# Taking an eighth of the edges' source rows from SBUF columns in every pair, and GpSimd's wait one gather later

## What is computed

```python
msg_in = concatenate([nodes[src], nodes[dst], edge_features], axis=-1)
messages = relu(msg_in @ mW1 + mb1) @ mW2 + mb2
aggregated = segment_sum(messages, dst)
upd_in = concatenate([nodes, aggregated], axis=-1)
out = layernorm(nodes + relu(upd_in @ uW1 + ub1) @ uW2 + ub2)
```

## Time and profile before

| | |
|---|---|
| median of three runs | 2489.68 us (2489.13 to 2490.9) |
| the profiled execution | 2490.1 us |
| its span in the profile | 2488.3 us |
| PE / PEld busy | 62% / 57% |
| POOL busy | 59% |
| DVE busy | 45% |
| ACT busy | 39% |
| granted TensorE clock, mean | 0.72 |

### The profile page before, as it was taken

How to read it: one execution, slowest core, us unless ns; L and a number is a source line. 1 busy time by engine, 2 the same in 40 slices (tenths; PEclk the granted TensorE clock), 3 DMA queues, 4 the chain that set the end, 5 groups by cost and what they waited for, 6 DMA issues and landing times. The chain is left out here.

```text
span 2488.3 us, 35326 instructions
## 1 busy us (share of the span) xinstructions
PE 1553.6 (62%) x8744; PEld 1428.1 (57%) x8744; DVE 1114.3 (45%) x4860; ACT 972.5 (39%) x6697; POOL 1475.7 (59%) x1576
## 2 busy tenths in 40 slices
PE   2676666665666666576666666567566566557657
PEld 2566655555565565565565565556566555556555
DVE  3435445444444444444444444444444444444443
ACT  1215334334334434443433433443433444443342
POOL 7155566666656666566666565665656666666653
PEclk6787776776766866766767777776766777676776
DMA  4634434333334333333333343343333343333331
GB/s 109 179 91 108 98 81 99 97 85 92 98 80 98 97 90 90 96 96 83 97 94 85 95 99 83 95 99 80 97 96 85 93 99 94 84 98 93 86 91 33
DMA packets 102736, 232.74 MB, mean 94 GB/s; under 512 B 47018, under 2 KB 63223, under 8 KB 89917
## 3 DMA queue, kind: packets, MB, share of 16 engines
q1 hardware_dynamic: 42532, 124.03, 19.9%
q0 software_dynamic: 49952, 100.83, 16.4%
q10 hardware_dynamic: 10046, 5.59, 0.9%
HBM read 220.66 MB, written 9.60 MB: 93 GB/s over the span
## 5 line engine op out<-in xcount | busy, mean ns | idle before, releaser
L797 POOL DMA_INDIRECT gath<-table_src,idx_all x1513 | 1427.6, 944 | 970.9 <-issue 873.0
L932 PE MATMUL ps_sum<-onehot,hid 128*128 128x96 f32 x3322 | 598.4, 353 | 628.0 <-ACT rhs L1065 535.8
L932 PEld LDWEIGHTS ps_sum<-onehot,hid 128*128 128x128 f32 x3322 | 563.4, 263 | 664.2 <-issue 659.8
L516 ACT COPY col_x<-xz 64x1 f32 x5960 | 634.9, 187 | 409.5 <-issue 403.9
L912 PE MATMUL ps_pre<-rhs,lhs 128*128 128x128 f32 x3226 | 593.7, 360 | 222.6 <-issue 164.3
L1298 DVE TENSOR_TENSOR hid<-ps_pre,gath 128x1024 f32<-128x1024 f32 x202 | 246.7, 1221 | 1067.3 <-DMA gath<-table_src,idx_all 925.6
L912 PEld LDWEIGHTS ps_pre<-rhs,lhs 128*128 128x128 f32 x3226 | 560.6, 270 | 244.1 <-issue 179.4
L1103 ACT ACTIVATE hid<-hid 128x1024 f32<-128x1024 f32 x202 | 212.7, 1053 | 358.9 <-DVE hid L1298 356.1
L539 DVE TENSOR_TENSOR col_x<-xz 64x2 int32 x3366 | 265.2, 148 | 81.5 <-issue 78.6
L1269 DVE TENSOR_SCALAR_CACHE_REDUCE lhs<-lhs,place 96x1024 f32<-96x1024 int32 x208 | 262.6, 1263 | 62.9 <-PE ps_sum L845 32.5
L1261 DVE TENSOR_TENSOR onehot<-ps_iota,dst_rel 128x768 f32<-128x768 f32 (+1 forms) x209 | 196.8, 942 | 0.1
(11 more groups left out here) (136 smaller groups left out, 672.6 us busy)
## 6 DMA issues: line engine op xcount, KB each, us to landing
lhs<-in_dst_dram SPq DMA_DIRECT2D x99, 768.0 KB
lhs<-in_edgeT_dram SPq DMA_DIRECT2D x98, 256.0 KB
gath<-table_src,idx_all POOLq DMA_INDIRECT x1513
table_src<-gath SPq DMA_DIRECT2D x12, 512.0 KB, 5.3
xwin<-in_xT_dram SPq DMA_DIRECT2D x208, 24.0 KB
lhs<-in_dst_dram SPq DMA_DIRECT2D x10, 384.0 KB
out_dram<-late_b ACTq DMA_DIRECT2D x48, 64.0 KB, 2.7
xz<-in_xT_dram ACTq DMA_DIRECT2D x4, 512.0 KB, 5.1
```

The costliest lines, as they stand in the source:

```text
L516: ins = copy(col_x[:, k, start + n + j:start + n + j + 1], col)
L797: pool.indirect_dma_start(gath[0:m, k, j * H:(j + 1) * H], None, table_src, src_by_tile(p, j, m)).then_inc(gathered[k], 16)
L932: nc.tensor.matmul(bank[:, 0:WIN], hid[0:m, k, j * H:(j + 1) * H], hot(k, j, m), start=(j == 0), stop=(m == TAIL or j == PT - 1))
```

## The change

Two edits. `COL_EVERY` becomes 1, so that each of the 197 pairs from 11 to 207 has one tile by columns and gathers only seven (the last pair three). All that depends on `has_cols(p)` follows from it: ACT copies 60 columns and DVE makes 34 joins in each step, the first 12 registers of the next pair are loaded by ACT behind the columns of the same step and ahead of `copy_window`, and the counts that semaphores are waited for go with them. And POOL now issues the first gather of a pair as soon as the slot is free; its wait for the gathers of the pair ahead stands between the first and the second gather.

```diff
-COL_EVERY = 2
+COL_EVERY = 1
...
-                if p > RAW:
-                    pool.wait_ge(gathered[(k - 1) % SLOTS], got(p - 1))
                 let(pool)
-                for j, m in tiles_of(p)[0:gathers_of(p)]:
+                for n, (j, m) in enumerate(tiles_of(p)[0:gathers_of(p)]):
+                    if n == 1 and p > RAW:
+                        pool.wait_ge(gathered[(k - 1) % SLOTS], got(p - 1))
+                        let(pool)
                     pool.indirect_dma_start(gath[0:m, k, j * H:(j + 1) * H], None, table_src, src_by_tile(p, j, m)).then_inc(gathered[k], 16)
```

## The result

The changed kernel took **2762.4 us** (2759.3 to 2777.6, four runs), the kernel before in the same comparison 2490.3 (2489.1 to 2495.5). The ratio is **1.109, interval 1.103 to 1.114**: slower by 272 us. The forecast was 2629.

A forecast was written before the change was run, and what follows sets the result against it. POOL was taken to set the pace now, ACT nearly as late; after the change ACT's step of 12.2 us replaces 11.49 over 196 steps, adding 139 us to 2490.1 for 2629 us. Range 2340 to 2780.

The forecast's parts named there:

- ACT sets the pace, slower than before: The forecast case: ACT's step of 12.2 us is longer than POOL's 9.5, DVE's and PE's; chance 0.59.
- the crawl: In ACT's batch, the slow supply of small instructions while gathers are in flight; 4.2 us of each batch.
- The marks named in advance: Signs in the profile after: slot releases POOL's first gather, relu hardly idle, 11,840 copies, batch near 10.6 us, relus 12.2 apart.
- the 10.6 forecast: ACT's batch of 60 column copies, busy and idle time together, taken from the profile before at 10.6 us.
- ACT's step: ACT's work per pair: batch 10.6, relu 1.06, `rhs` copy 0.16, node update 0.4; sum 12.2 us.
- the quarter of a node update: Term of ACT's step: L1152 at 0.47 and squares about 1.0, a quarter of them a pair, 0.4 us.
- a register load priced at 0.74 us: Upper cost of ACT's moved load of the next pair's first 12 registers; step 12.95 us, time 2776.
- The register load taken at 0: ACT's load of the next pair's first 12 registers, behind queued copies ahead of the `rhs` copy, costs 0.
- The wait edit "is worth nothing" if ACT sets the pace: With ACT setting the pace, POOL waits for the slot, not the landing, so moving its wait gains nothing.
- Register-addressed columns whose registers are not loaded yet come slowly: Inference for ACT's batch while gathers are in flight: nine columns took 0.6 us each, the others about 0.1.
- the rival given 0.09, POOL keeps the pace: If the crawl nearly vanishes, ACT's step is 9.6 us, POOL's 9.5, and time 2118 us; chance 0.09.
- the 0.78 worked out: What stays of POOL's 2.03 us wait once the first gather (1.25 us) runs inside it: 0.78 us.

The follow-up runs named there:

- Fixed columns: The changed kernel, but ACT copies its 60 columns from fixed places of xz and loads no registers for them; 2070.3 us without the crawl, 2751.2 with it.
- every other pair, no wait: The kernel before without POOL's wait for the landings of the preceding pair's gathers, columns still in every other pair; 2906.5 us, ratio 1.171, with the crawl.
- wait only: The changed kernel with columns in every other pair, so that only POOL's wait is moved; 2207.5 us, ratio 0.883, without the crawl.
- cols only: The kernel before with columns in every pair, POOL's wait left ahead of a pair's first gather; 2331.6 us, ratio 0.930, without the crawl.
- no wait: The changed kernel without POOL's wait for the gathers of the pair ahead, only the free slot gating; 1859.4 us, ratio 0.744, without the crawl.

## Why the prediction was right, and by what it was right

**ACT sets the pace, slower than before: right, and with luck,** in both comparisons with the crawl (ratios 1.109 and 1.120). The marks named in advance are there: the slot as releaser of POOL's first gather, a relu without idle time ahead, 11,840 copies, a batch of 10.98 us against the 10.6 forecast. The luck is that the comparison had the crawl, like the profile that the forecast was made from; in the two later ones without it in which it ran, the changed kernel was faster than the kernel before by 17 to 18%.

**The size was short by 133 us**, against the profiled 2777.6 by 149. The step of the sum that was mis-sized is ACT's step, 12.97 us for 12.2, and 196 x 0.77 = 151. Half is the batch: + 0.38. The other half is the quarter of a node update, forecast at 0.4: ahead of L1153 and L1161, ACT is idle for 23.9 + 29.5 us, 0.35 us a pair, mostly with a releaser that the profile can't name. The upper end of the range, 2780, held the time by 18 us, and it stood for another cause: a register load priced at 0.74 us, which the runs don't show.

**The register load taken at 0: right.** Without the crawl a batch with five loads and 60 registers takes 5.66 us with no idle time that can be seen in it, and kernels whose ACT loads none in the loop cost the same (2070 and 2078 beside 2065). The trace also records the loads themselves, which the views leave out: the five of a batch take 3.99 us together, 66 ns a register, with the crawl as without it, and run beside the copies. The Trainium skill ("Runtime: NRT & Kernel Launch", section "Instruction fetch mechanics") gives some 200 ns a register, in a remark on the loads that the runtime adds. The prediction carried it over to these loads from a table in SBUF, where 60 would take 12 us; the 3.99 us show that it does not hold for them.

**The wait edit "is worth nothing" if ACT sets the pace: not shown, and perhaps too kind.** The moved wait was not run alone with the crawl. But the whole wait taken away from the kernel before cost 428 us there: the pause at each landing was worth more to the other engines than it cost POOL, and no term of the sum held that.

**What failed is a premise:** that the crawl in the one profile of before belongs to the kernel. "Register-addressed columns whose registers are not loaded yet come slowly" was inferred from coinciding times. `Fixed columns` with the crawl shows that it is neither ACT's register loads nor its addressing, and PE in `every other pair, no wait` that it isn't ACT alone. And three of the five later comparisons had no crawl. There the rival given 0.09, POOL keeps the pace at 2118 us, is what happened, at 2061 to 2065, and its sums hold: `wait only` was to save 1.25 us a pair, 245 us, and saved 291; `cols only` was to come to 10.77 us a pair and came to 11.1 (1006 gathers in 1600 us are 143.7 pairs). The rest of the wait is 1.05 to 1.25 us idle, 0.30 of it the usual gap, so 0.75 to 0.95 for the 0.78 worked out.

**Why before's time hid it.** With the crawl the kernel before took 2478 and 2490 us, without it 2498 to 2503. POOL's chain of gathers and landings was its bound either way, and ACT's 10.6 us batch fitted beside it in two steps. But the near-equal times are two differences that cancel. With the crawl the start is slower: the first relu with columns comes at 184.95 us, without it at 116.88, 68 us sooner. And the steady stretch is quicker: 172 relus in 2000 us, 11.63 us a pair, for 167 and 11.98. The gathers cost POOL 7.5 x 1.248 = 9.36 us of either, so a landing was waited for some 0.3 us longer without the crawl; why, no run shows. The change takes POOL's wait and ACT's empty step together, so that the time becomes that of ACT: 12.97 us a pair where a batch crawls, 9.75 (POOL again) where it takes 5.66.

**What stays open** is how the crawl works and what makes it come and go; nothing in the programs provoked it. One candidate is the supply of instructions. They come by DMA: the two instruction queues moved 1.73 + 1.26 = 2.99 MB for 46,113 instructions, 65 bytes each. The Trainium skill (the same page and section) says that each sequencer fetches its next block through a DMA queue of its own while it executes the current one. One might argue from it that gathers crowd out these fetches, so that an engine slows once its block is used up. For that speaks that the crawl begins late: in the earlier trace rows 4.6 us after a burst starts (gathers from 1508.72, the first gap ahead of 1513.79), and ACT, after 15.84 us of rest, still makes 18 copies at full speed 20.6 us into the burst of `every other pair, no wait`.

The trace of the result speaks against it. From 1508.9 ACT's copies come in bunches of one to four, and then it makes 49 at full speed. Here are these 49, and all that DMA did from 1508.6 to 1517.6:

```profile
1513.17 4.68 ACT L516 COPY col_x<-xz 64x1 f32 x49 [0.51 <-issue]
...
DMA packets 128, 0.26 MB, mean 29 GB/s; under 512 B 64, under 2 KB 64, under 8 KB 128
...
q0 software_dynamic: 128, 0.26, 10.6%
```

The gathers alone, at a tenth of the engines' time, and no packet of an instruction queue: by these records, what ended this crawl was not the landing of instructions. Between 400 and 2400 us the trace has 105 such crawls (three or more bunches of under eight copies in a row). In 47 of them no instruction packet moved, and in only 4 did one end in the last microsecond ahead of the quick copies. These begin instead, in the median, 2.5 us after the start of the last gather. So a crawl ends with the burst of gathers, and by what they hold up the other engines is open. A run with gathers spaced out, or spread over more queues, in the presence of the crawl would tell more; none was made.

The fastest kernel, `no wait`, took 1859 us without the crawl. With the crawl it was not run, and its sibling with columns in every other pair was slower than before by 17%, so it isn't shown to beat the kernel before everywhere.

## What to carry to other kernels

When a profile shows idle time in bunches with no releaser, take a second profile at another time before you forecast from it: a kernel bound elsewhere keeps nearly the same time while one of its engines takes twice as long for its batch (10.6 us for 5.7), and the change that makes that engine the bound shows it. And equal totals don't show equal runs: compare the start and the steady pace each by itself. A wait that looks like pure loss on the bound engine can be the break that others recover in; price it at both ends. And an edit that takes away two covers at once, POOL's wait and ACT's empty step here, should be measured with each alone and at more than one time.

## What the runs showed of the hardware

- The same program, 2762 and 2768 us in two comparisons, 2065 and 2061 in two others. With the crawl, instructions of ACT and DVE come in bunches of one to four every 0.71 us or a multiple, or one matmul in 2.1 to 3.5 us, from some 4.5 us or more into a burst of gathers. They are at full speed again 2.5 us (median of 105) after the last gather of the burst starts.
- Without it, 60 copies of 64 x 1 with register addresses take 5.66 us, 94 ns each, with the loads of the registers beside them: 3.99 us for 60 registers in five loads, 66 ns each.
- GpSimd's indirect gathers of 128 rows can follow each other without end at 1.25 us (1042 in 1300 us). Waiting for the landing before the next pair costs 2.0 us in the two pairs of the earlier trace rows and 2.4 in `cols only` without the crawl (11.13 - 7 x 1.248), behind the first gather 0.75 to 0.95.
